# Expert rows stored in order and gathered per token, in place of scattered to their tokens, in a four-layer kernel on one core

## The chip, the cores and the metric

The kernel runs on one core of a Trainium2 chip. The metric is the device time of one execution in microseconds (us), the median of several runs. The engines are PE (matrix multiply, TensorE), DVE (VectorE), ACT (ScalarE), POOL (GpSimd) and SP (SyncE, here only an issuer of DMAs). Plain DMAs are issued by SP. DMAs that take row numbers from a tile (indirect DMAs) are issued by POOL.

## The reference, cut to what matters

4096 tokens of 256 values pass six steps, each with a residual. The change is in the first three mixtures (steps 1, 3 and 4).

```
x = x + 0.5 * MoE0(layernorm(x))     # 1
x = x + attention(layernorm(x))      # 2
x = x + 0.5 * MoE0(layernorm(x))     # 3
x = x + 0.5 * MoE1(layernorm(x))     # 4
x = x + mixer(layernorm(x))          # 5
x = x + 0.5 * MoE1(layernorm(x))     # 6
# MoE0: T = 4096 tokens, E = 8 experts; each takes its first T/E = 512 tokens, others get 0
idx = argmax(probs); locations = cumsum(mask) - mask; mask = mask * (locations < 512)
exp_out = einsum(exp_in, W) + b      # exp_in[e, c] is the token in slot c of expert e
out[token] = probs[token, idx] * exp_out[idx, its slot]
# MoE1: every token goes to expert e = argmax(gates)
h = gelu(x @ W1[e] + b1[e]); out = h @ W2[e] + b2[e]
```

## The kernel before, in words

All tokens stay in SBUF as `X` (128 partitions x 32 tiles x 256). Each of the six steps, here called stages, first makes layer norms of them, and the mixtures also choose experts (`pe_route`, `act_route`, `dve_route`, `pool_route`). In a route, DVE computes for each group of 8 tiles the slot number of every token, and POOL then sends the group's normalised rows to a DRAM area `moe0_slots` or `moe1_slots`, one indirect DMA per tile of 128 tokens (line L543, 32 of them per route). With each row go its token number and, for the last stage, its mean and deviation: two small POOL copies per group (L540, L541), so that a row is 259 wide.

In the expert stages (`*_moe0(r)`, `*_moe1(m)`), SP loads pairs of tiles from the slots into a ring of five (`rows`), PE transposes and multiplies, ACT and DVE move results, and DVE writes a pair of result tiles into a ring of three (`expert_out`, L678 and L862). MoE 0 has 16 pairs, MoE 1 has 20. POOL takes each pair as it is done and scatters it by the token numbers in the loaded rows to `expert_rows` in DRAM, one indirect DMA per tile (L716, semaphores `back0` to `back2`). The scatter's arrival frees both rings: SP loads pair j only when pair j - 5 is back (L570, L738), DVE writes pair n only when pair n - 3 is back. Slots that no token took hold a spare row number. For this the slots are filled from a tile `EMPTY` before each MoE 0: by SP at the start (L1560), and for the second time by way of an area `moe0_empty_slots` (stores L583, copied at L907 during attention). `expert_rows` is zeroed at L558.

When all pairs are back, SP (`sp_rows_back`, L608 to L612) reads `expert_rows` plainly into `normed` in five pieces of 4, 4, 8, 8 and 8 tiles (`y_in0` to `y_in4`). DVE of the next stage adds a tile times its gate to `X` (L287) just ahead of that tile's statistics (L308), so the first tiles can be worked on while the later ones land. It takes the statistics in groups: 4 tiles, then 8, 8, 8 and 4, or (4, 8, 4) in attention.

Each engine has its own program in order. At each stage's end every engine adds one to `stage_end`, and some steps of the next stage wait for all five:

- attention: only SP's loads of its weights (L892) and POOL. ACT and DVE then wait for the weights (`att_in`) to make `W1R` (L1101, L1184), and the projections (L980) follow.
- route2 (after the second MoE 0): ACT before the first copy of logits (L421, L422, `stage_end` 15).
- mixer: SP, ACT and DVE at their very beginning (L1385, L1442, L1489, `stage_end` 20).

Of the kernel before, what the change touches and what calls it, by code (L numbers as in the profile page):

```python
# [15 lines left out]
P = 128  # L16
# [82 lines left out]
def tiles_of(ap):  # L99
# [25 lines left out]
def plan(nc, a, out):  # L125
# [29 lines left out]
    k.SLOT = m.take("slot_of_token", [P, NT], I32)  # L155
    k.CE = m.take("tile_counts", [P, 4, E])
# [39 lines left out]
def plan_moe0(m, first):  # L196
    t = Names()
    t.LT = m.take("logits_T", [E, 3, 2 * P])
    t.WT = m.take("w0", [P, KD, E, D])
    t.BB = m.take("b0", [P, E, D])  # L200
    t.XS = m.take("rows", [P, RING_X, 2, RW])
    t.XST = m.take("rows_T", [P, 3, 2, KD, P])
    t.YS = m.take("expert_out", [P, 3, 2, D])
    t.EMPTY = m.take("empty", [P, NT, RW]) if first else None
    return t


def plan_moe1(m):
# [4 lines left out]
    t.XS = m.take("rows", [P, RING_X, 2, RW])  # L213
    t.HS = m.take("hidden", [P, 3, 2, D])
    t.YS = m.take("expert_out", [P, 3, 2, D])
    return t
# [63 lines left out]
def dve_add(k, stage, t):  # L280
# [4 lines left out]
    if t == CUTS[c][0]:  # L285
        nc.vector.wait_ge((s.y_in0, s.y_in1, s.y_in2, s.y_in3, s.y_in4)[c], 16 * n)
# [141 lines left out]
def dve_route(k, r):  # L428
# [18 lines left out]
    if r < 2:  # L447
# [75 lines left out]

def pool_route(k, r):
    nc, s = k.nc, k.s
    slots = k.slots0 if r < 2 else k.slots1
    number = k.XN[:, :, D:D + 1].bitcast(I32)[:, :, 0]
    if r == 1:
        nc.gpsimd.wait_ge(s.stage_end, 5 * 2)
        nc.gpsimd.wait_ge(s.slots_empty, 16)  # L530
    elif r == 2:
        nc.gpsimd.wait_ge(s.split_lo, 2 * KD)
    k.ps.step(nc.gpsimd.iota(number, pattern=[[P, NT]], base=0, channel_multiplier=1, allow_small_or_imprecise_dtypes=True))
    if r == 0:
        nc.gpsimd.wait_ge(s.emptied, 16 * E)
    for g in range(NG):
# [3 lines left out]
        nc.gpsimd.tensor_copy(k.XN[:, lo:hi, D + 1], k.MV[:, lo:hi, 0])  # L540
        k.ps.step(nc.gpsimd.tensor_copy(k.XN[:, lo:hi, D + 2], k.SD[:, lo:hi]))  # L541
        for t in range(lo, hi):
            nc.gpsimd.indirect_dma_start(out=slots, out_offset=bass.IndirectOffsetOnAxis(ap=k.SLOT[:, t:t + 1], axis=0),  # L543
                                         in_=k.XN[:, t, :], in_offset=None).then_inc(s.scattered, 16)
# [5 lines left out]
def sp_moe0(k, r):  # L550
# [6 lines left out]
    if r == 0:  # L557
        nc.sync.dma_start(tiles_of(k.y_rows[0:T, :]), t.EMPTY[:, :, 0:D]).then_inc(s.y0_zeroed, 16)  # L558
# [5 lines left out]
    back = (s.back0, s.back1, s.back2)  # L564
    pairs = NJ0 // 2
    for n in range(-3, pairs):
        j = n + 3
        if j < pairs:
            if j >= RING_X:
                nc.sync.wait_ge(back[(j - RING_X) % 3], back_count(r, j - RING_X))  # L570
# [10 lines left out]
        if r == 0 and n >= 0 and n % 2:  # L581
            cut = slice(n // 2 * NT * 2 // pairs, (n // 2 + 1) * NT * 2 // pairs)
            nc.sync.dma_start(tiles_of(k.empty0)[:, cut, :], t.EMPTY[:, cut, :]).then_inc(s.empty_stored, 16)  # L583
            if n == 1:
                nc.sync.dma_start(tiles_of(k.slots1[SPARE:SPARE + (NJ1 - NT) * P, :]),
                                  t.EMPTY[:, E:E + NJ1 - NT, :]).then_inc(s.spares_stored, 16)
    sp_rows_back(k, r)
    if r == 0:
        nc.sync.wait_ge(s.empty_stored, 16 * (pairs // 2))
        nc.sync.wait_ge(s.spares_stored, 16)  # L590
# [78 lines left out]
def dve_moe0(k, r):  # L669
    nc, s, t = k.nc, k.s, k.top0[r]  # L670
    back = (s.back0, s.back1, s.back2)
# [16 lines left out]
def pool_moe0(k, r):  # L688
    nc, s, t = k.nc, k.s, k.top0[r]
    xs_in = (s.xs_in0, s.xs_in1, s.xs_in2, s.xs_in3, s.xs_in4)  # L690
    pairs, at = NJ0 // 2, r * NJ0 // 2
    if r == 0:
# [9 lines left out]
        nc.gpsimd.wait_ge(s.y0_zeroed, 16)  # L702
    else:
        for sem in (s.y_in0, s.y_in1, s.y_in2, s.y_in3, s.y_in4):
            nc.gpsimd.wait_ge(sem, 16)
# [6 lines left out]
def pool_rows_back(k, t, n, to):  # L712
    nc, s = k.nc, k.s
    back = (s.back0, s.back1, s.back2)
    for i in range(2):
        nc.gpsimd.indirect_dma_start(  # L716
            out=to, out_offset=bass.IndirectOffsetOnAxis(ap=t.XS[:, n % RING_X, i, D:D + 1].bitcast(I32), axis=0),
            in_=t.YS[:, n % 3, i, :], in_offset=None).then_inc(back[n % 3], 16)
# [5 lines left out]
def sp_moe1(k, m):  # L724
    nc, s, t = k.nc, k.s, k.top1[m]
    xs_in = (s.xs_in0, s.xs_in1, s.xs_in2, s.xs_in3, s.xs_in4)
    back = (s.back0, s.back1, s.back2)
    nc.sync.wait_ge(s.pads_from, m + 1)
    for e in range(E):
        row = nc.sync.value_load(k.PADI[0:1, e:e + 1], min_val=0, max_val=SPARE - P)  # L730
        nc.sync.dma_start(k.slots1[bass.ds(row, P), :], k.PAD[:, e:e + RW]).then_inc(s.padded, 16)
# [4 lines left out]
    for j in range(NJ1 // 2):  # L736
        if j >= RING_X:
            nc.sync.wait_ge(back[(j - RING_X) % 3], back_count(m + 2, j - RING_X))  # L738
        for i in range(2):
            row = nc.sync.value_load(k.ROWI[0:1, 2 * j + i:2 * j + i + 1], min_val=0, max_val=SPARE + (NJ1 - NT - 1) * P)  # L740
            nc.sync.dma_start(t.XS[:, j % RING_X, i, :], k.slots1[bass.ds(row, P), :]).then_inc(xs_in[j % RING_X], 16)
    if m == 0:
        sp_rows_back(k, 2)
# [93 lines left out]
def dve_moe1(k, m):  # L837
# [5 lines left out]
    for n in range(pairs + 4):  # L843
        j = n - 4
        if 0 <= j < pairs:
            ys = t.YS[:, j % 3, :, :]
            bank = k.bank[6 + j % 2]
            if j >= 3:
                nc.vector.wait_ge(back[j % 3], back_count(m + 2, j - 3))
# [25 lines left out]
def pool_moe1(k, m):  # L875
    nc, s, t = k.nc, k.s, k.top1[m]
# [842 lines left out]
```

## Time and profile before

| | us |
|---|---|
| median of 3 runs | 1552.46 |
| the three runs | 1542.86, 1554.94, 1552.46 |
| the profiled execution, its own time | 1545.96 |
| its span, from the first to the last instruction | 1544.7 |
| PE, DVE, ACT, POOL busy | 1147.4, 973.6, 813.9, 606.7 |
| mean granted PE clock, as a share of full speed | 0.881 |

The chain of work that ended last is spread over many lines, since each stage has a bound of its own. The stages lie, in the span: route0 to 80 us, MoE 0 to 141, attention to about 920, route1 to 983, MoE 0 again to 1045, route2 to 1127, MoE 1 to 1247, mixer to 1350, route3 and MoE 1 again to the end. Work after 1350 is not touched by the change except for the DRAM area that it uses.

### The profile page before, as it was taken

The numbers are of one execution on the slowest core, as the hardware profiler recorded it, in microseconds if no ns is written. First come the engines' busy times: TensorE is split into PE (matmuls) and PEld (weight loads), VectorE is DVE, ScalarE is ACT, GpSimd is POOL, SyncE is SP. The second block draws the span as 40 slices with busy tenths as digits, with TensorE's granted clock in tenths as the row PEclk, the third lists the DMA queues.
The fourth block names the chain that finished last, engine by engine and source line by source line (L and its number), as shares of the span: only waits on it lengthen the run. The fifth ranks groups of instructions, "written<-read, shape, count | busy, mean of one in ns | idle before, by whom it ended". The sixth has DMA issues, their size and how long they took to land. (4 is left out here: it accounts for less than half of the span.)

```text
span 1544.7 us, 30156 instructions
## 1 busy us (share of the span) xinstructions
PE 1147.4 (74%) x12088; PEld 898.3 (58%) x12088; DVE 973.6 (63%) x1669; ACT 813.9 (53%) x907; POOL 606.7 (39%) x610
## 2 busy tenths in 40 slices
PE   4464789199999989649999967463669928973998
PEld 2253666188888886448888853352258814631786
DVE  4213745799999954689999984137424447743454
ACT  4311453499999804279999956134323324471332
POOL 2753000825545410435454445560723311335233
PEclk9888799699999999869999989696779968975898
DMA  9578101312122000101221221463333240013232
GB/s 293 217 220 251 44 1 34 135 57 85 56 84 82 31 8 1 58 28 57 84 80 61 84 79 70 149 219 116 114 90 101 90 147 0 1 41 129 66 101 79
DMA packets 84588, 140.55 MB, mean 91 GB/s; under 512 B 10574, under 2 KB 71246, under 8 KB 79956
## 3 DMA queue, kind: packets, MB, share of 16 engines
q1 hardware_dynamic: 71396, 102.76, 20.7%
q0 software_dynamic: 13056, 35.87, 6.5%
q8 instruction: 99, 1.62, 0.4%
q14 instruction: 37, 0.30, 0.1%
HBM read 86.60 MB, written 56.24 MB: 92 GB/s over the span
## 5 line engine op out<-in xcount | busy, mean ns | idle before, releaser
L1167 ACT ACTIVATE b_signs<-b_q_everywhere,normed 128x2048 bf16<-128x2048 f32 x224 | 432.7, 1993 | 32.0 <-PE bank L1077 27.2
L1077 PE MATMUL bank<-b_value_parts,b_signs 128*128 128x102 bf16 x8192 | 408.0, 209 | 36.5 <-DVE b_signs L1308 26.7
L1077 PEld LDWEIGHTS bank<-b_value_parts,b_signs 128*128 128x128 bf16 x8192 | 378.3, 97 | 73.3 <-DVE b_signs L1308 70.6
L1308 DVE TENSOR_SCALAR b_signs<-b_q_everywhere,normed 128x2048 bf16<-128x2048 f32 x288 | 390.7, 1392 | 1.9 <-PE bank L1077 1.9
L543 POOL DMA_INDIRECT moe_slots<-normed,slot_of_token x128 | 124.8, 975 | 39.3 <-issue 33.5
L1369 POOL TENSOR_TENSOR normed<-b_sums,normed 128x16 f32<-128x16 f32 x32 | 34.8, 1087 | 249.4 <-DVE b_sums L1319 249.4
L359 PE MATMUL bank<-identity,normed 128*128 128x128 f32 x256 | 51.6, 338 | 63.2 <-ACT normed L335 46.9
L1345 POOL TENSOR_TENSOR b_signs<-b_signs,normed 128x1024 f32<-128x1024 f32 x8 | 22.0, 2756 | 160.8 <-DVE normed L1258 160.3
L308 DVE BATCH_NORM_STATS2 ln_stats<-residual 128x6 f32<-128x256 f32 x192 | 73.8, 419 | 17.8 <-DMA bg<-in_bg 7.7
L1069 PE MATMUL bank<-normed,ones_bf 128*128 128x408 bf16 x128 | 28.9, 350 | 69.5 <-DVE normed L1276 69.5
L368 PE MATMUL bank<-normed_T,wg 128*8 128x256 f32 x256 | 75.9, 425 | 0.0
L359 PEld LDWEIGHTS bank<-identity,normed 128*128 128x128 f32 x256 | 33.6, 168 | 71.9 <-ACT normed L335 52.2
L1319 DVE TENSOR_REDUCE b_sums<-bank 128x136 f32<-128x408 f32 x128 | 72.5, 570 | 2.3 <-PE bank L1077 2.3
L716 POOL DMA_INDIRECT out_tokens<-f_expert_out,f_rows x40 | 38.4, 961 | 89.2 <-DVE f_expert_out L858 83.1
L716 POOL DMA_INDIRECT expert_rows<-d_expert_out,d_rows x40 | 38.9, 972 | 82.5 <-DVE d_expert_out L862 76.4
L335 ACT ACTIVATE normed<-residual,ln_shift,ln_rstd 128x256 f32<-128x256 f32 x128 | 68.6, 586 | 2.1 <-DVE ln_shift L330 2.1
L323 ACT ACTIVATE ln_std<-ln_mean_var,eps 128x4 f32<-128x4 f32 (+1 forms) x32 | 9.4, 293 | 109.7 <-DVE ln_mean_var L311 109.7
L1069 PEld LDWEIGHTS bank<-normed,ones_bf 128*128 128x128 bf16 x128 | 10.9, 99 | 75.8 <-DVE normed L1276 70.3
L678 DVE TENSOR_TENSOR a_expert_out<-bank,a_b 128x512 f32<-128x512 f32 x16 | 11.1, 692 | 63.3 <-PE bank L639 61.8
L1371 POOL TENSOR_TENSOR normed<-b_sums,normed 128x256 f32<-128x256 f32 x32 | 50.8, 1588 | 0.0
L872 DVE TENSOR_TENSOR f_rows_T<-bank,f_rows_T 128x512 fp32r<-128x512 f32 x20 | 13.8, 692 | 57.7 <-ACT f_rows_T L833 57.7
L1130 ACT ACTIVATE b_q_or_k_T<-bank 128x512 fp32r<-128x512 f32 x32 | 17.6, 595 | 60.1 <-PE bank L1006 60.1
(246 smaller groups left out, 2431.4 us busy)
## 6 DMA issues: line engine op xcount, KB each, us to landing
b_q_everywhere<-q_rows SPq DMA_DIRECT2D x32, 1024.0 KB, 4.7
normed<-expert_rows SPq DMA_DIRECT2D x9, 1024.0 KB, 10.3
d_rows<-moe_slots SPq DMA_DIRECT2D x40, 129.5 KB, 2.1
f_rows<-moe_slots SPq DMA_DIRECT2D x40, 129.5 KB, 2.1
moe_slots<-a_empty SPq DMA_DIRECT2D x8, 518.0 KB, 8.4
a_rows<-moe_slots SPq DMA_DIRECT2D x16, 259.0 KB, 3.6
moe_empty_slots<-a_empty SPq DMA_DIRECT2D x8, 518.0 KB, 5.3
moe_slots<-moe_empty_slots SPq DMA_DIRECT2D x1, 4144.0 KB
```

The source lines that it names most:

```text
L308: marks.append(k.vs.mark(nc.vector.bn_stats(k.STATS[:, t % 8, :], k.X[:, t, :])))
L335: return k.nc.scalar.activation(dst, k.X[:, t, :], ACT.Identity, bias=k.SHIFTS[:, t:t + 1], scale=k.RSTD[:, t:t + 1])
L359: ins = nc.tensor.transpose(k.bank[n % 3][:, (2 * c + i) * P:(2 * c + i + 1) * P], k.XN[:, 2 * n + i, c * P:(c + 1) * P], k.IDENT[:, :])
L368: ins = nc.tensor.matmul(k.bank[3 + p % 2][0:E, 0:2 * P], wg[:, c, :], k.XTR[:, p % 3, :, :, :].rearrange("p i k c -> p (i k c)")[:, c * 2 ...
L543: nc.gpsimd.indirect_dma_start(out=slots, out_offset=bass.IndirectOffsetOnAxis(ap=k.SLOT[:, t:t + 1], axis=0), in_=k.XN[:, t, :], in_offse ...
L716: nc.gpsimd.indirect_dma_start(out=to, out_offset=bass.IndirectOffsetOnAxis(ap=t.XS[:, n % RING_X, i, D:D + 1].bitcast(I32), axis=0), in_= ...
L1069: nc.tensor.matmul(bank[:, 0:QPB * VP].rearrange("p (i c) -> p i c", i=QPB), k.ONESB[:, :], t.HELD3[:, h, :].unsqueeze(1).broadcast_to([P, ...
L1077: ins = nc.tensor.matmul(banks[qt // QPB][:, qt % QPB * VP:(qt % QPB + 1) * VP], t.SG[:, (hh * TB + kt) % RING, qt * P:(qt + 1) * P], t.VO ...
L1167: nc.scalar.activation(t.SG[:, g % RING, :], t.QB[:, hh % 2, :], ACT.Sign, bias=t.NKT[:, kt, hh % H:hh % H + 1]).then_inc(s.sign_a, 1)
L1308: nc.vector.tensor_scalar(t.SG[:, g % RING, :], t.QB[:, hh % 2, :], t.KTM[:, kt, hh % H:hh % H + 1], 2.0, ALU.is_gt, ALU.mult).then_inc(s. ...
L1319: nc.vector.tensor_reduce(t.A[:, hh % 2, QPB * c:QPB * (c + 1), :], k.bank[4 * (hh % 2) + c][:, 0:QPB * VP].rearrange("p (i n c) -> p i c ...
L1371: step(nc.gpsimd.tensor_tensor(t.CT, t.A[:, r, :, 0:DH], q.unsqueeze(2).broadcast_to([P, TB, DH]), ALU.mult))
```

## The change

In the first three mixtures, SP stores each pair of result tiles plainly, one pair behind the other, to `moe0_rows` or `moe1_rows` (semaphores `stored0` to `stored2`). `rows` in the ring is freed when PE has transposed it, `expert_out` when its store has landed. DVE computes for every token the row where its result stands (`FROM`: two more operations in MoE 0, four in MoE 1). When all pairs are stored, POOL reads the rows back by these numbers, one indirect DMA per tile of tokens, 32 of them. They stand in POOL's program ahead of its `stage_end`. The last mixture still scatters to the output as before. Token numbers, means and deviations are written to the slots in the last route only, so rows are 256 wide elsewhere. Zeroing of `expert_rows`, the area of empty slots and its copy are gone, and `EMPTY` has 8 tiles in place of 32.

```diff
-    for n in range(-3, pairs):
-        j = n + 3
+    for n in range(-RING_X, pairs):
+        if n >= 0:
+            nc.sync.wait_ge(s.ys, at + n + 1)
+            nc.sync.dma_start(tiles_of(k.y0[2 * n * P:2 * (n + 1) * P, :]), t.YS[:, n % 3, :, :]).then_inc(stored[n % 3], 16)
+        j = n + RING_X
         if j < pairs:
             if j >= RING_X:
-                nc.sync.wait_ge(back[(j - RING_X) % 3], back_count(r, j - RING_X))
+                nc.sync.wait_ge(s.xs_turned, at + j - RING_X + 1)
...
-def sp_rows_back(k, m):
+def pool_rows_back(k, m, rows, where):
     nc, s = k.nc, k.s
-    for sem, n in zip((s.back0, s.back1, s.back2), back_all(m)):
-        nc.sync.wait_ge(sem, n)
+    for i, sem in enumerate((s.stored0, s.stored1, s.stored2)):
+        nc.gpsimd.wait_ge(sem, stored_count(m, max(j for j in range((NJ0, NJ0, NJ1)[m] // 2) if j % 3 == i)))
     if m == 1:
-        nc.sync.wait_ge(s.split_lo, 2 * KD)
+        nc.gpsimd.wait_ge(s.split_lo, 2 * KD)
     for sem, (lo, hi) in zip((s.y_in0, s.y_in1, s.y_in2, s.y_in3, s.y_in4), CUTS):
-        nc.sync.dma_start(k.XN[:, lo:hi, 0:D], tiles_of(k.y_rows[lo * P:hi * P, :])).then_inc(sem, 16)
+        for t in range(lo, hi):
+            nc.gpsimd.indirect_dma_start(out=k.XN[:, t, 0:D], out_offset=None, in_=rows,
+                                         in_offset=bass.IndirectOffsetOnAxis(ap=where[:, t:t + 1], axis=0)).then_inc(sem, 16)
...
 def pool_moe0(k, r):
-    for n in range(pairs):
-        nc.gpsimd.wait_ge(xs_in[n % RING_X], xs_count(r, n))
-        nc.gpsimd.wait_ge(s.ys, at + n + 1)
-        pool_rows_back(k, t, n, k.y_rows)
+    nc.gpsimd.wait_ge(s.rows_from, r + 1)
+    pool_rows_back(k, r, k.y0, k.FROM)
...
 def dve_moe0(k, r):
         if n >= 3:
-            nc.vector.wait_ge(back[n % 3], back_count(r, n - 3))
+            nc.vector.wait_ge(stored[n % 3], stored_count(r, n - 3))
...
 def pool_route(k, r):
-        nc.gpsimd.tensor_copy(k.XN[:, lo:hi, D + 1], k.MV[:, lo:hi, 0])
-        k.ps.step(nc.gpsimd.tensor_copy(k.XN[:, lo:hi, D + 2], k.SD[:, lo:hi]))
+        if r == 3:
+            nc.gpsimd.tensor_copy(k.XN[:, lo:hi, D + 1], k.MV[:, lo:hi, 0])
+            k.ps.step(nc.gpsimd.tensor_copy(k.XN[:, lo:hi, D + 2], k.SD[:, lo:hi]))
...
 def sp_attention(k):
-        if batch == 0:
-            nc.sync.dma_start(k.by_slot, k.empty0.rearrange("(e r) d -> e r d", e=E)).then_inc(s.slots_empty, 16)
```

## Rows read from the trace of the kernel before

**Rows 1.** Stretches of the two MoE 0 stages: busy us of each engine, clock, DMA share, GB/s.

```profile
91.10:136.30 45.20, 33.67 (x171) 26.34 (x169) 10.36 (x16) 9.32 (x15) 28.30 (x30) 1.00 0.79 244
991.80:1040.00 48.20, 34.87 (x171) 27.51 (x169) 19.50 (x19) 16.46 (x19) 33.09 (x29) 0.96 0.63 204
```

**Rows 2.** Waits, whole span: us in total, times, longest.

```profile
PE bank L627 <- DMA a_rows<-moe_slots: 36.8, 12, 26.3
...
SPq L572 <- DMA expert_rows<-a_expert_out,a_rows: 32.8, 10, 9.4
```

**Rows 3.** Timeline of first MoE 0: start, us, instruction [idle before].

```profile
90.44 0.69 DVE L678 TENSOR_TENSOR a_expert_out<-bank,a_b 128x512 f32<-128x512 f32 x1 [28.45 <-PE bank L639]
...
92.30 0.60 PE L627 MATMUL bank<-identity,a_rows 128*128 128x128 f32 x4
...
94.47 0.60 PE L627 MATMUL bank<-identity,a_rows 128*128 128x128 f32 x4
...
135.65 0.69 DVE L678 TENSOR_TENSOR a_expert_out<-bank,a_b 128x512 f32<-128x512 f32 x1 [1.45 <-DMA expert_rows<-a_expert_out,a_rows]
```

**Rows 4.** Timeline of POOL in route0, between two groups of scatters.

```profile
68.16 0.97 POOL L543 DMA_INDIRECT moe_slots<-normed,slot_of_token  x1 [0.31 <-issue]
69.13 0.21 POOL L540 COPY normed<-ln_mean_var 128x8 f32<-128x8 f32 x1
69.27 0.20 POOL L541 COPY normed<-ln_std 128x8 f32<-128x8 f32 x1
69.74 0.99 POOL L543 DMA_INDIRECT moe_slots<-normed,slot_of_token  x1 [0.28 <-POOL normed L541]
```

**Rows 5.** DMA issues of whole span: KB each, median us to landing.

```profile
a_rows<-moe_slots SPq DMA_DIRECT2D x16, 259.0 KB, 3.6
moe_empty_slots<-a_empty SPq DMA_DIRECT2D x8, 518.0 KB, 5.3
...
normed<-in_w SPq DMA_DIRECT2D x4, 1024.0 KB, 6.5
...
moe_slots<-pad_source SPq DMA_DIRECT2D x16, 129.5 KB, 2.5
...
e_scalars<-in_mix SPq DMA_DIRECT2D x1, 0.5 KB, 6.1
```

**Rows 6.** Timeline of SP, ACT and DVE where attention begins.

```profile
147.13 3.04 SPq L894 DMA_DIRECT2D b_wq<-in_wq  x1
...
169.69 0.69 DVE L1184 TENSOR_TENSOR b_hidden_weights<-b_q_everywhere,b_hidden_weights 128x512 fp32r<-128x512 f32 x1 [5.91 <-ACT b_hidden_weights L1101]
```

**Rows 7.** Timeline of SP and of ACT where the mixer and the sign steps begin.

```profile
1253.82 2.43 SPq L1386 DMA_DIRECT2D e_w_in<-in_win_t  x1
...
1259.20 0.43 SPq L1391 DMA_DIRECT2D e_scalars<-in_mix  x1
...
308.17 5.79 ACT L1167 ACTIVATE b_signs<-b_q_everywhere,normed 128x2048 bf16<-128x2048 f32 x3 [1.44 <-DVE b_value_parts L1268]
```

**Rows 8.** Timeline of second MoE 0 and route2, engine by engine.

```profile
1002.98 2.38 POOL L716 DMA_INDIRECT expert_rows<-c_expert_out,c_rows  x1 [0.59 <-issue]
...
1083.63 1.05 POOL L543 DMA_INDIRECT moe_slots<-normed,slot_of_token  x1 [0.30 <-issue]
...
991.09 0.69 DVE L678 TENSOR_TENSOR c_expert_out<-bank,c_b 128x512 f32<-128x512 f32 x1 [26.73 <-PE bank L639]
...
1002.23 2.29 DVE L684 TENSOR_TENSOR w_lo<-normed,w_hi 128x2048 fp32r<-128x2048 f32 x1
...
1039.35 0.69 DVE L678 TENSOR_TENSOR c_expert_out<-bank,c_b 128x512 f32<-128x512 f32 x1 [1.03 <-PE bank L639]
...
1068.53 0.37 ACT L422 ACTIVATE d_logits_T<-bank 8x256 f32<-8x256 f32 x1 [1.07 <-PE bank L368]
```

**Rows 9.** The tile of MoE 1's results: duration ns, first and last start.

```profile
L862 DVE COPY d_expert_out<-bank x20: 691/691/692, 1144.3 to 1242.6; 128x512 f32<-128x512 f32 x20
```

**Rows 10.** The chain that ended last, where the mixer begins.

```profile
1253.83 0.44 DVE residual L287
```

More of the change, by code:

```diff
@@ L155, in plan @@
     k.SLOT = m.take("slot_of_token", [P, NT], I32)
+    k.FROM = m.take("row_of_token", [P, NT], I32)
     k.CE = m.take("tile_counts", [P, 4, E])
@@ L200, in plan_moe0, with plan_moe1 @@
     t.BB = m.take("b0", [P, E, D])
-    t.XS = m.take("rows", [P, RING_X, 2, RW])
+    t.XS = m.take("rows", [P, RING_X, 2, D])
     t.XST = m.take("rows_T", [P, 3, 2, KD, P])
     t.YS = m.take("expert_out", [P, 3, 2, D])
-    t.EMPTY = m.take("empty", [P, NT, RW]) if first else None
+    t.EMPTY = m.take("empty", [P, NJ1 - NT, RW]) if first else None
     return t
-def plan_moe1(m):
+def plan_moe1(m, width):
     t = Names()
@@ L212, in plan_moe1 @@
     t.HT = m.take("hidden_T", [P, 2, 3, 2, KD, P], F32R)
-    t.XS = m.take("rows", [P, RING_X, 2, RW])
+    t.XS = m.take("rows", [P, RING_X, 2, width])
     t.HS = m.take("hidden", [P, 3, 2, D])
@@ L453, in dve_route @@
         k.vs.step(nc.vector.tensor_scalar(k.r_keep[:, :], k.r_slot[:, :], float(E * REGION + CAP), None, ALU.is_lt))
+        k.vs.step(nc.vector.tensor_scalar(k.r_slot[:, :], k.r_slot[:, :], float(E * REGION + CAP - 1), float(E * (CAP - REGION)),
+                                          ALU.min, ALU.add))
+        nc.vector.scalar_tensor_tensor(out=k.FROM[:, :], in0=k.r_rank[:, :], scalar=-float(CAP), in1=k.r_slot[:, :],
+                                       op0=ALU.mult, op1=ALU.add).then_inc(s.rows_from, 1)
         k.vs.step(nc.vector.tensor_tensor(k.r_gate[:, :], k.r_gate[:, :], k.r_keep[:, :], ALU.mult))
@@ L670, in dve_moe0 @@
     nc, s, t = k.nc, k.s, k.top0[r]
-    back = (s.back0, s.back1, s.back2)
+    stored = (s.stored0, s.stored1, s.stored2)
     pairs, at = NJ0 // 2, r * NJ0 // 2
@@ L688, in pool_moe0 @@
 def pool_moe0(k, r):
-    nc, s, t = k.nc, k.s, k.top0[r]
-    xs_in = (s.xs_in0, s.xs_in1, s.xs_in2, s.xs_in3, s.xs_in4)
-    pairs, at = NJ0 // 2, r * NJ0 // 2
+    nc, s = k.nc, k.s
     if r == 0:
@@ L727, in sp_moe1 @@
     back = (s.back0, s.back1, s.back2)
+    pairs, at = NJ1 // 2, m * NJ1 // 2
     nc.sync.wait_ge(s.pads_from, m + 1)
@@ L735, in sp_moe1 @@
     nc.sync.wait_ge(s.stage_end, 5 * (3, 5)[m])
[L736 to L743, printed above, removed]
+    for n in range(-RING_X, pairs):
+        if m == 0 and n >= 0:
+            nc.sync.wait_ge(s.m_ys, n + 1)
+            nc.sync.dma_start(tiles_of(k.y1[2 * n * P:2 * (n + 1) * P, :]), t.YS[:, n % 3, :, :]).then_inc((s.stored0, s.stored1, s.stored2)[n % 3], 16)
+        j = n + RING_X
+        if j < pairs:
+            if j >= RING_X and m == 0:
+                nc.sync.wait_ge(s.m_turned, j - RING_X + 1)
+            elif j >= RING_X:
+                nc.sync.wait_ge(back[(j - RING_X) % 3], back_count(j - RING_X))
+            for i in range(2):
+                row = nc.sync.value_load(k.ROWI[0:1, 2 * j + i:2 * j + i + 1], min_val=0, max_val=SPARE + (NJ1 - NT - 1) * P)
+                nc.sync.dma_start(t.XS[:, j % RING_X, i, :], k.slots1[m][bass.ds(row, P), :]).then_inc(xs_in[j % RING_X], 16)
 def pe_moe1(k, m):
@@ L847, in dve_moe1 @@
             bank = k.bank[6 + j % 2]
-            if j >= 3:
-                nc.vector.wait_ge(back[j % 3], back_count(m + 2, j - 3))
+            if j >= 3 and m == 0:
+                nc.vector.wait_ge((s.stored0, s.stored1, s.stored2)[j % 3], stored_count(2, j - 3))
+            elif j >= 3:
+                nc.vector.wait_ge(back[j % 3], back_count(j - 3))
             if m == 1:
@@ L876, in pool_moe1 @@
     nc, s, t = k.nc, k.s, k.top1[m]
+    if m == 0:
+        nc.gpsimd.wait_ge(s.rows_from, 3)
+        pool_rows_back(k, 2, k.y1, k.FROM)
+        return
     xs_in = (s.xs_in0, s.xs_in1, s.xs_in2, s.xs_in3, s.xs_in4)
-    pairs, at = NJ1 // 2, m * NJ1 // 2
-    for sem in (s.y_in0, s.y_in1, s.y_in2, s.y_in3, s.y_in4):
-        nc.gpsimd.wait_ge(sem, 32)
-    for n in range(pairs):
-        nc.gpsimd.wait_ge(xs_in[n % RING_X], xs_count(m + 2, n))
-        nc.gpsimd.wait_ge(s.m_ys, at + n + 1)
-        pool_rows_back(k, t, n, k.out if m else k.y_rows)
+    back = (s.back0, s.back1, s.back2)
+    for n in range(NJ1 // 2):
+        nc.gpsimd.wait_ge(xs_in[n % RING_X], xs_count(3, n))
+        nc.gpsimd.wait_ge(s.m_ys, NJ1 // 2 + n + 1)
+        for i in range(2):
+            nc.gpsimd.indirect_dma_start(
+                out=k.out, out_offset=bass.IndirectOffsetOnAxis(ap=t.XS[:, n % RING_X, i, D:D + 1].bitcast(I32), axis=0),
+                in_=t.YS[:, n % 3, i, :], in_offset=None).then_inc(back[n % 3], 16)
 def sp_attention(k):
@@ L1572, in sp_program @@
     sp_moe1(k, 1)
-    for sem, n in zip((s.back0, s.back1, s.back2), back_all(3)):
-        nc.sync.wait_ge(sem, n)
+    for i, sem in enumerate((s.back0, s.back1, s.back2)):
+        nc.sync.wait_ge(sem, back_count(max(j for j in range(NJ1 // 2) if j % 3 == i)))
 def pe_program(k):
```

93 lines of the change are left out of this document (39 added, 54 removed).

## The prediction

> **What bounds the kernel now.** I read the stretches first, then the waits, then the timelines of the three expert stages that the change touches and of what comes behind each. In both MoE 0 stages PE is busy for 33.7 and 34.9 us of 45.2 and 48.2 us, at nearly its full clock, and the DMA engines are 0.79 and 0.63 busy [rows 1]. So neither is the bound. The waits say what is: PE waits for loaded rows, and SP, which loads them, waits for scattered rows to come back [rows 2]. Where the rows are there, pairs follow each other at 94.47 - 92.30 = 2.17 us [rows 3]; from the first to the last result pair the stage takes 136.34 - 91.13 = 45.2 us for 15 steps, 3.01 us each [rows 3]. In the second MoE 0 it is 1040.04 - 991.78 = 48.3 us [rows 8]. Two scatters of 0.97 us with 0.31 us between them [rows 4] are 2.55 us per pair, more than PE's 2.17. In MoE 1 the pairs come at (1242.6 - 1144.3) / 19 = 5.17 us [rows 9], twice what POOL needs for its two scatters, so there nothing but the last pair is in the open.
>
> The change takes the scatter out of the loop and puts 32 gathers behind it, in front of a `stage_end`. So I must price the loops, and then the path from the last result to the first step that the gathers hold up. I take the stages one by one, each against the time of before.
>
> **Routes 0, 1 and 2.** The number, mean and deviation copies go. Between two groups POOL then needs 0.31 us in place of 69.74 - 69.13 = 0.61, and before the first group, by my estimate, 0.7 us less to do (two copies and their wait): three times 0.3 and 0.7 are 1.6 us in each route, as POOL works through all 32 scatters without a pause for slots. In route2 one group waits for its slots, so 1.4 there. Rows of 1024 in place of 1036 bytes change nothing, since POOL's own time sets the pace. The zeroing of `expert_rows` and the smaller `EMPTY` lie beside the scatters of route0, and the copy of empty slots lies in attention before the first sign step, which starts at 308.17 and waits for DVE and not for a DMA [rows 7]. I cost them at nothing; were that cover gone, the copy would be worth some 10 us of gain. DVE's two and four extra operations for `FROM` run while POOL scatters.
>
> **First MoE 0.** PE's pace becomes 2.17 us if the rest keeps up. Load n + 5 is now issued behind store n. It lands about 0.9 us (two issues) plus 3.6 us [rows 5] after result n, and PE needs it some 5.5 us after, so there is room. DMA traffic is 7 MB in 33 us, 215 GB/s, under the 244 / 0.79 = 309 that the engines showed [rows 1]. I take 2.2 us: 33.0 in place of 45.2 us. From the last result to the last store's landing I take 3.6 us. No such store is in the trace: 128 rows of 1 KB land in 2.5 us, 518 KB in 5.3 [rows 5]; the store is 256 KB, nearer to the first.
> Then 32 gathers. The trace has no gather. Its nearest row is the scatter, also 128 row numbers and 1 KB each: 0.97 + 0.31 = 1.28 us [rows 4], so 31 x 1.28 + 0.97 and a drain of 0.3 are 41.0 us. Below, a gather might be as cheap as a plain issue on SP, 0.43 us [rows 7], with the 0.31 between; above, 2.38 us, what a scatter took when DVE's 2.29 us operation ran beside it [rows 8]. I take the scatter, as it is the same kind of instruction.
> Who waits? ACT and DVE may start on the first tiles, which arrive early: 16 tiles have landed 16 x 1.28 + 2.5 = 23 us after the first gather, and ACT and DVE, by the order of their work before, are done with them some 16 us later, 39 us in all. But SP queues attention's eight loads behind `stage_end`, and ACT's and DVE's weight steps L1101 and L1184 need them. Six such loads for the mixer took 1259.63 - 1253.82 us to issue and 6.1 us to land, 11.9 us, with plain reads in front of them [rows 5, 7]; I take 11.5, and 0.7 for ACT. That is now the last: 33.0 + 3.6 + 41.0 + 11.5 + 0.7 = 89.8 us from the first result to L1184. Before it was 169.69 - 91.13 = 78.6 [rows 3, 6]. Loss 11.2, less 1.6 from route0: +9.6.
>
> **Second MoE 0.** Here SP also loads four raw weight pieces of 1 MB, 6.5 us each [rows 5]. Before, the first was issued ahead of the loop, since n ran from -3. Now it is issued behind result 1, and ACT wants it with pair 4, about 6.5 us later, while it lands 7.5 us or more after result 1 among stores and loads. Each piece then holds ACT (1.9 us of its own) and DVE (2.29, [rows 8]) up, and the next one is issued later. Following the four pieces I get 7.7 to 9 us per three pairs, in all 41 us in place of 48.3. Bounds: 33 us (PE's pace) and 48.3 (no gain).
> The waiting step behind the gathers is ACT's copy of logits in route2, before at 1068.53 [rows 8]: 76.8 us after the first result. Now: 41 + 3.6 + 41.0 = 85.6, +8.9. By then DVE has done the statistics of tiles 12 to 19, on which it was working before at that moment: -1.0. PE has stood idle and starts at half clock: +0.5. Routes: -1.6 and -1.4. Sum +5.4.
>
> **First MoE 1.** The loop stays PE's. Before, 10.5 us passed from the last result (1242.6 + 0.7) to the mixer's first step at 1253.83 [rows 9, 10], which waits for `stage_end`. Now 3.6 + 41.0 = 44.6 us. ACT, DVE and SP all wait there, so nothing of the gathers is hidden: +34.1.
>
> **Sum.** 9.6 + 5.4 + 34.1 = 49 us on the profiled execution's own time of 1545.96 (its span is 1544.7): 1595. The median of the three runs is 1552.46, 6.5 higher; on it the sum gives 1601.5. I predict 1600.
>
> **A rule of the skill beside it.** A 2.29 us DVE operation lengthened a scatter from 0.97 to 2.38 us; beside DVE's adds and statistics of route2 one took 1.05 [rows 8]. The Trainium skill, "GPSIMD Engine Reference", section "Key points", says that GpSimd shares its SBUF interfaces with VectorE and meets contention from instructions with two SBUF inputs; DVE's adds are such. If each of the 36 adds that run during the gathers of stages 1 and 3 cost a gather its own 0.47 us, the sum would be 17 us higher, near 1617. The row with 1.05 speaks for 3 us at most, and I leave it out.
>
> **Rivals.**
> *A gather is cheap* (not slower). If POOL hands over one description per tile and not 128 rows, a gather may cost what an issue on SP costs, 0.43 us, or 0.74 with the pause. Then each stage saves 32 x 0.54 = 17 us: 49 - 52 = -3, or 1550 on the median. The change decides between faster and slower at a step of 1.28 - 49/96 = 0.77 us. Against it: the scatter, with as many row numbers, is at 0.97 to 1.05 wherever DVE's long operation isn't beside it [rows 4, 8]. For it: only that the direction differs. Chance 0.06.
> *A gather is dear*: every one meets something like the 2.38 us scatter. 96 x 1.41 = 135 us more: about 1735. Half of that, 1670, would need contention on every second. In the mixer's case DVE is idle, which speaks against it. Chance 0.10. The Trainium skill's "GPSIMD Engine Reference", section "Performance pitfalls for Q7 kernels", has a harsher price, about 102 cycles for each small read command, such as one per gather index, not overlapped. It would apply to 128 indices, 13,000 cycles or some 10 us a gather, an estimate by that page, and 900 us in all. The scatter's 0.97 us for as many indices goes against it; I give it 0.01 of the 0.10.
> *The loops don't get faster*: loads queued behind stores come as late as scatters did before, and the pace stays 3.01 and 3.2 us. Loss 12.2 + 7.3: 49 + 19.5 = 69, about 1621. For it: the DMA engines were 0.79 busy, and SP is now in series behind result n. Against: the empty slots, 4 MB of the traffic, are gone. Chance 0.12.
>
> **How the numbers follow.** My forecast has 0.72. Its own range: cheaper by 8 (second MoE 0 at PE's pace), 3 (three stores at 2.5 us) and 2 (weight loads): +36; dearer by 2 for weight loads that queue as before, and 5 for stores at 5.3: +56. With the rival of the unchanged loops: +75. That is 1582 to 1621 on the profiled time and, with 6.5 for the median, up to 1628. The range 1582 to 1628 leaves out the cheap and the dear gather, 0.16. About 1 per cent is what a measurement of this kernel can tell from no change. Faster by over 1 per cent: only a gather well below the cheap rival's, 0.02. Within 1 per cent: 0.05. Slower: 0.93.
>
> **What would show it.** In the changed trace: POOL with three rows of 32 gathers at a step of 1.28 us, each followed by `stage_end`; results of the first MoE 0 at 2.2 us; ACT, DVE and PE idle for about 45 us ahead of the mixer; attention's weights landing some 11 us behind the last gather; w_hi steps that wait for raw weights. The prediction is wrong if a gather's step isn't near 1.28, or if the loops gain more than PE's pace allows, which they can't, or if a drain on POOL waits for data too, some 2 us per stage.

## The result and the profile after

The changed kernel takes 1606.6 us (median of 4 runs, 1604.6 to 1610.0), the kernel before 1552.3 (1542.9 to 1554.9): a ratio of 1.036, with a 95% interval of 1.032 to 1.040. The forecast was 1600 and slower. The profiled executions lie towards opposite ends of the spread (1610.0, the slowest after, and 1545.96, 6.5 under the median before), so their spans, 1608.5 and 1544.7, are 63.8 us apart where the medians are 54 apart.

The stretches of the changed kernel: first MoE 0 and second MoE 0 from the end of the first result to the end of the last, which answer to [rows 1], and the third from the last result of the first MoE 1 to the mixer's first add.

```profile
90.25:127.65 37.40, 33.34 (x171) 28.32 (x169) 10.38 (x15) 9.29 (x15) 0.00 (x0) 0.95 0.77 239
1004.78:1044.65 39.87, 34.09 (x171) 28.18 (x169) 18.99 (x19) 16.16 (x19) 0.00 (x0) 0.96 0.84 271
1273.89:1322.21 48.32, 0.00 (x0) 0.00 (x0) 0.00 (x2) 0.00 (x0) 30.52 (x32) 0.50 0.31 92
```

The loops fell from 45.2 to 37.4 and from 48.3 to 39.9 us, with POOL idle in them. In the third row POOL alone works, 30.5 us in 32 gathers of 48.3 us. The gathers as a group of the page, and DMA issues with their landing (the rows that answer to [rows 5]):

```profile
L630 POOL DMA_INDIRECT normed<-moe_rows,row_of_token x96 | 93.1, 970 | 260.3 <-DMA moe_rows<-d_expert_out 127.1
...
moe_rows<-d_expert_out SPq DMA_DIRECT2D x20, 256.0 KB, 2.2
...
moe_rows<-a_expert_out SPq DMA_DIRECT2D x16, 256.0 KB, 2.4
...
moe_rows<-c_expert_out SPq DMA_DIRECT2D x16, 256.0 KB, 3.8
...
normed<-moe_rows,row_of_token POOLq DMA_INDIRECT x96, 2.8
```

A gather is busy 0.97 us and lands 2.8 us after its issue. The Trainium skill, "Perfetto Trace Analysis", section "DMA Instruction — SWDGE (GPSIMD)", says that such an instruction ends in a profile when its descriptors are written, not when the data has moved; these two rows agree.

The timeline of the changed kernel from the last result of the first MoE 0 to attention's weights (it answers to [rows 3] and [rows 6]):

```profile
126.96 0.69 DVE L697 TENSOR_TENSOR a_expert_out<-bank,a_b 128x512 f32<-128x512 f32 x1 [1.04 <-PE bank L658]
130.59 0.99 POOL L630 DMA_INDIRECT normed<-moe_rows,row_of_token  x1 [49.97 <-DMA moe_rows<-a_expert_out]
131.89 0.96 POOL L630 DMA_INDIRECT normed<-moe_rows,row_of_token  x1 [0.30 <-issue]
...
170.38 0.95 POOL L630 DMA_INDIRECT normed<-moe_rows,row_of_token  x1 [0.30 <-issue]
176.66 0.37 SPq L909 DMA_DIRECT2D b_wq<-in_wq  x1
...
180.11 0.42 SPq L913 DMA_DIRECT2D b_bv<-in_bv  x1
...
183.39 0.63 ACT L1114 ACTIVATE b_hidden_weights<-b_q_everywhere 128x512 fp32r<-128x512 f32 x1 [14.99 <-DMA b_bv<-in_bv]
184.06 0.69 DVE L1197 TENSOR_TENSOR b_hidden_weights<-b_q_everywhere,b_hidden_weights 128x512 fp32r<-128x512 f32 x1 [21.01 <-ACT b_hidden_weights L1114]
```

The last gather ends at 171.33, but SP's first load, which waits for `stage_end`, goes out at 176.66, 5.3 us later. No instruction of any engine stands between: the chain puts this time down to POOL's drain (L1675). It comes again behind the other two rows of gathers:

```profile
1088.77 0.95 POOL L630 DMA_INDIRECT normed<-moe_rows,row_of_token  x1 [0.30 <-issue]
1095.10 0.37 ACT L423 ACTIVATE d_logits_T<-bank 8x256 f32<-8x256 f32 x1 [14.45 <-POOLq L1680]
...
1273.20 0.69 DVE L872 COPY d_expert_out<-bank 128x512 f32<-128x512 f32 x1 [3.74 <-PE bank L813]
...
1276.92 0.98 POOL L630 DMA_INDIRECT normed<-moe_rows,row_of_token  x1 [127.10 <-DMA moe_rows<-d_expert_out]
...
1315.93 0.95 POOL L630 DMA_INDIRECT normed<-moe_rows,row_of_token  x1 [0.30 <-issue]
1322.21 0.42 DVE L288 SCALAR_TENSOR_TENSOR residual<-normed,residual 128x256 f32<-128x256 f32 x1 [48.32 <-POOLq L1683]
```

5.4 us at ACT's first logits (they answer to 1068.53 in [rows 8]) and 5.3 us at the mixer's first add ([rows 10]). And the timeline of the first MoE 0 of the changed kernel where its pace breaks:

```profile
93.26 0.50 SPq L605 DMA_DIRECT2D moe_slots<-a_empty  x1
...
96.21 1.24 SPq L605 DMA_DIRECT2D last_slots<-a_empty  x1
98.12 0.69 DVE L697 TENSOR_TENSOR a_expert_out<-bank,a_b 128x512 f32<-128x512 f32 x1 [1.47 <-PE bank L658]
100.28 0.69 DVE L697 TENSOR_TENSOR a_expert_out<-bank,a_b 128x512 f32<-128x512 f32 x1 [1.47 <-PE bank L658]
105.82 0.69 DVE L697 TENSOR_TENSOR a_expert_out<-bank,a_b 128x512 f32<-128x512 f32 x1 [4.84 <-DMA moe_rows<-a_expert_out]
```

Results come every 2.16 us; then 5.5 us pass. I put this down to the stores and loads that queue behind two stores of spare rows, 1 MB each, which SP issues behind results 1 and 2 (counted from 0); a run below moves them away.

Where the 63.8 us between the spans lie (us; each row runs from the mark of the row above to its own):

| up to | before | after | difference | forecast |
|---|---|---|---|---|
| first result of MoE 0 (end) | 91.1 | 90.3 | -0.9 | -1.6 |
| DVE's weights of attention (L1184, now L1197) | 78.6 | 93.8 | +15.2 | +11.2 |
| first result of the second MoE 0 | 822.1 | 820.7 | -1.4 | -1.6 |
| ACT's first logits of route2 | 76.8 | 90.3 | +13.6 | +8.9 |
| first result of MoE 1 | 76.4 | 78.4 | +2.0 | -1.9 |
| its last result | 98.4 | 100.4 | +2.0 | 0 |
| the mixer's first add | 10.5 | 48.3 | +37.8 | +34.1 |
| the end | 290.9 | 286.3 | -4.6 | 0 |

### The profile page after: what moved, and what is told of

Same layout as the page of the kernel before. It is cut to its first block, busy times and chain, and to the rows that moved or that the text cites. A ratio compares the mean times of both kernels' runs of the same rounds, so it can differ in the third digit from the quotient of the medians.

```text
span 1608.5 us, 30095 instructions
## 1 busy us (share of the span) xinstructions
PE 1149.6 (71%) x12088; PEld 903.6 (56%) x12088; DVE 975.3 (61%) x1677; ACT 813.7 (51%) x907; POOL 584.1 (36%) x575
## 4 chain that ended last, share of the span: by engine, by line
PE 34%; DVE 32%; POOL 15%; issue 6%; POOLq 4%; DMA 4%; ACT 4%; SPq 1%; DVEq 0%; ACTq 0%
DVE b_signs L1321 21%; POOL moe_slots L563 5%; DVE b_sums L1332 4%; PE bank L810 4%; POOL normed L630 4%; PE bank L658 3%; PE bank L811 3%; PE bank L812 2%; PE bank L813 2%; PE bank L993 2%; PE bank L1090 2%; PE bank L1044 2%; DVE ln_stats L309 2%; POOL last_slots L563 2%; PE bank L1434 2%
## 5 line engine op out<-in xcount | busy, mean ns | idle before, releaser
L630 POOL DMA_INDIRECT normed<-moe_rows,row_of_token x96 | 93.1, 970 | 260.3 <-DMA moe_rows<-d_expert_out 127.1
L563 POOL DMA_INDIRECT moe_slots<-normed,slot_of_token x96 | 93.5, 974 | 102.8 <-DVE slot_of_token L499 74.5
L1422 PE MATMUL bank<-identity,normed_T 128*128 128x128 f32 x64 | 11.6, 319 | 70.5 <-ACT normed_T L336 70.4
L288 DVE SCALAR_TENSOR_TENSOR residual<-normed,r_gate,residual 128x256 f32<-128x256 f32 x64 | 30.2, 471 | 37.2 <-DMA normed<-moe_rows,row_of_token 37.2
L1422 PEld LDWEIGHTS bank<-identity,normed_T 128*128 128x128 f32 x64 | 8.3, 160 | 74.3 <-ACT normed_T L336 73.4
```

The lines of the kernel that those rows point to most:

```text
L630: nc.gpsimd.indirect_dma_start(out=k.XN[:, t, 0:D], out_offset=None, in_=rows, in_offset=bass.IndirectOffsetOnAxis(ap=where[:, t:t + 1], a ...
```

## The experiments

Each ran in several rounds beside the kernel before on the same chip, and ratios are to it, with 95% intervals. Four chips were used: A for the first four kernels (kernel before 1551.9 us), B for the next four (1572.4), C for the next three (1570.5), D for the last (1548.7). B and C are slower by more than a per cent; more on this below. Of all versions only the kernel before ran on all four, so a ratio on one chip set against a ratio on another can hold a difference of the chips.

**The gate ahead of the gathers.**

```diff
 def pool_rows_back(k, m, rows, where):
...
+    nc.gpsimd.drain().then_inc(s.stage_end, 1)
     for sem, (lo, hi) in zip(...):
...
     pool_moe0(k, 0)
-    nc.gpsimd.drain().then_inc(s.stage_end, 1)
```

> The changed kernel with one thing moved, in all three stages: POOL's drain and its stage_end stand behind the waits for the stores and ahead of the 32 gathers. Theory A (the gathers cost so much since a stage_end stands behind them, and a drain): attention's weights, route2's logits and the mixer start as soon as the stores have landed. I expect 14 us less ahead of attention, 14 ahead of route2 and 31 ahead of the mixer, 1606.6 - 59 = 1548 us, within 0.5 per cent of the kernel before. If the drain costs its 5.3 us also where no indirect DMA ran shortly before, 16 us more: 1564. Theory B (the rows come late whatever the gate does, since one gather takes 1.26 us and DVE waits for 16 tiles): less than 20 us gained, above 1586.

Measured: 1573.2 us, ratio 1.016 (1.013 to 1.018). 33 us of the loss went with the place of the gate: `stage_end` had held steps up that need none of the gathered rows. That is between the two theories, for two reasons. The drain costs something here too: in the first MoE 0, 5.7 us passed from the last result's end to the first gather (126.99 to 132.70), and 2.9 in the changed kernel. The length of the drain itself stands on its line, 2.65 and 2.68 us in the two MoE 0 stages and 5.26 in MoE 1:

```profile
L626 POOLq DRAIN  x3: 2651/2680/5264, 129.2 to 1251.7; - x3
```

And what the gate lets go meets the gathers' own pace. The chief row of waits for the add:

```profile
DVE residual L288 <- DMA normed<-moe_rows,row_of_token: 66.3, 9, 15.1
```

In the changed kernel the same row has 37.2 us.

**A no-operation in place of the drain.** In it POOL's sequencer runs ahead of the engine, so `stage_end` is no longer behind the gathers.

```diff
     pool_moe0(k, 0)
-    nc.gpsimd.drain().then_inc(s.stage_end, 1)
+    nc.gpsimd.nop().then_inc(s.stage_end, 1)
```

> The changed kernel with a nop in place of each of the three drains that stand behind the gathers; nothing else. Theory A: the 5.3 us from the end of the last gather to stage_end are the drain's own, so 3 x 5.3 = 16 us go: 1591 us. Rival: POOL's queue gives the signal no sooner than the last gather's descriptors or data are done with, whatever instruction carries it: 1606, no change.

Measured: 1562.0 us, ratio 1.009 (1.006 to 1.011). Far more than either theory gave, as both took the signal for one that comes behind the last gather. SP's first load and DVE's weights among the gathers:

```profile
153.54 0.37 SPq L909 DMA_DIRECT2D b_wq<-in_wq  x1
153.78 0.95 POOL L630 DMA_INDIRECT normed<-moe_rows,row_of_token  x1 [0.30 <-issue]
...
157.95 0.43 SPq L918 DMA_DIRECT2D b_sums<-in_bk  x1
...
166.37 0.69 DVE L1197 TENSOR_TENSOR b_hidden_weights<-b_q_everywhere,b_hidden_weights 128x512 fp32r<-128x512 f32 x1 [5.91 <-ACT b_hidden_weights L1114]
```

The signal came at 153.5, between gathers 20 and 21 (the last starts at 168.19): 12 gathers ahead of the end, and so it was in the MoE 1 stage. DVE's weights came at 166.37 in place of 184.06, ACT's first logits at 1063.27 in place of 1095.10. The drain's price isn't gone, though: the next drain, at the end of attention, was 0.04 us long in the changed kernel and is 5.30 here, 745 us behind the last gather. Nothing waits for it there: from DVE's weights to the first scatter of route1 it took 770.5 us here and 769.5 in the changed kernel.

**MoE 0 alone.** The first MoE 1 scatters as before (`out_offset` by the token number, the ring freed by `back`), the two MoE 0 stages store and gather.

> The change in the two MoE 0 stages alone; the first MoE 1 scatters its rows by token number and reads them plainly, as before (rows of 259 with their number there). Theory A: ahead of the mixer nothing of the gathers was hidden and nothing gained, so all of the 37.8 us that the trace shows there go, and 2 us of the loop: 1606.6 - 39 = 1567 us. Theory B (the mixer would have waited for its rows or weights anyway): less than 20 us less, above 1586.

Measured: 1568.8 us, ratio 1.012 (1.009 to 1.014). A is right: of 3.6% loss the MoE 1 stage holds 2.5, or 38 us, where the table has +37.8 for the way to the mixer's first add.

**Spare rows stored in route0.**

```diff
     if r == 0:
         for n in range(2):
+            nc.sync.dma_start(tiles_of(k.slots1[n][SPARE:...]), t.EMPTY[...]).then_inc(s.spares_stored, 16)
...
-        if r == 0 and n in (1, 2):
-            spares = tiles_of(k.slots1[n - 1][SPARE:...])
```

> The changed kernel with the two stores of spare rows (2 MB) issued in route0, ahead of the first MoE 0's loop, in place of between its stores and loads. Theory A: these two transfers made the one stall of the loop (4.8 us before the result at 105.8), and without them pairs come at 2.17 us from first to last, 33 in place of 37.4 us: 1602 us. Rival: the stall is the loop's own (a store waits its turn behind loads whatever else is queued): still there, 1606.

Measured: 1600.4 us, ratio 1.032 (1.029 to 1.035). A is right. The loop went from 88.29 to 120.24, 32.0 us: PE's pace without a break.

**The kernel before without the drain's price.** The same edit as above, three times, in the kernel before. The timeline and the chain of the kernel before, where the mixer begins:

```profile
1247.84 5.54 SPq L612 DMA_DIRECT2D normed<-expert_rows  x5
...
1253.83 0.43 DVE L287 SCALAR_TENSOR_TENSOR residual<-normed,residual 128x256 f32<-128x256 f32 x1 [10.49 <-POOLq L1676]
```

```profile
1246.34 1.52 issue
1247.86 5.94 POOLq L1676
```

> The kernel before with one edit: POOL still waits for all scattered rows, but a plain no-operation, not a drain, adds to stage_end behind the first three mixtures. Theory A (a drain on POOL behind indirect DMAs costs about 5.9 us of its own, although the rows are back): it stands ahead of attention's weights, of route2's first logits and of the mixer, so up to 3 x 5.9 = 18 us go: 1534 to 1541. Rival B (the 5.9 us are time in which the data still settles, or other work hides the drain in the two MoE 0 stages): 1546 to 1552.

Measured: ratio 0.999 (0.996 to 1.002). B's number, by its second reason, and in all three stages: other work lies beside the drain. The same rows without the drain:

```profile
1269.25 5.55 SPq L612 DMA_DIRECT2D normed<-expert_rows  x5
1274.89 0.43 DVE L287 SCALAR_TENSOR_TENSOR residual<-normed,residual 128x256 f32<-128x256 f32 x1 [10.14 <-SPq L1569]
```

SP's five plain reads take 5.5 us to issue, and SP's own signal stands behind them. The wait is put down to SP now and is as long, 10.1 for 10.5 us. In the two MoE 0 stages it is alike: from the last result to attention's weights 33.4 us passed with the drain and 33.1 without, to ACT's first logits in route2 28.5 and 28.5. All three drains can be read in the trace of before, on their own lines:

```profile
L1664 POOLq DRAIN  x1: 5293/5293/5293, 141.2 to 141.2; - x1
...
L1666 POOLq DRAIN  x1: 34/34/34, 917.2 to 917.2; - x1
...
L1671 POOLq DRAIN  x1: 5274/5274/5274, 1045.7 to 1045.7; - x1
...
L1676 POOLq DRAIN  x1: 5933/5933/5933, 1247.9 to 1247.9; - x1
```

So the drain was there before, of about the same size, and free; the change took away the reads that covered it. As above, the no-operation only put the price off: the drain at the end of attention (L1666) took 5.29 us without the first of them, where it hid as well.

**Plain reads of the stored rows.** The 96 gathers are left out, and SP reads the areas in five pieces, in the experts' order.

```diff
-        for t in range(lo, hi):
-            nc.gpsimd.indirect_dma_start(out=k.XN[:, t, 0:D], ...)
+        nc.sync.dma_start(k.XN[:, lo:hi, 0:D], tiles_of(rows[lo * P:hi * P, :])).then_inc(sem, 16)
```

> The changed kernel without its 96 gathers: SP reads the stored rows plainly in five pieces, as before, so the rows stay in the experts' order and the output is another one. It prices the rest of the change alone. Theory A (the loops gain what the traces show): 1552 - 4.6 (routes) - 7.8 and - 8.4 (the two MoE 0 loops) - 15 (POOL's drain now stands behind nothing) = 1516, and the gathers with their drains then cost 1606 - 1516 = 90 us. Rival B (the loops' gain is given back where rows are read back, since stores and plain reads queue behind one another): 1535 or more.

Measured: ratio 0.984 (0.981 to 0.987), 26 us on 1572, between the two. The loops gave what A took (37.4 and 40.6 us from the first result's start to the last's, against 46.5 and 47.9 in the kernel before with the no-operation, on the same chip): 16 us. A's 15 for POOL's drain weren't there, as the run above shows. So the gathers and what waits for them cost some 1.0364 - 0.9837 = 5.3%, 82 us, and the loops and routes give 26 back; the first ratio is from another chip than the second.

**A wait for the data, then the drain.**

```diff
+    for sem, (lo, hi) in zip((s.y_in0, s.y_in1, s.y_in2, s.y_in3, s.y_in4), CUTS):
+        nc.gpsimd.wait_ge(sem, 16 * (hi - lo) * (m + 1))
     nc.gpsimd.drain().then_inc(s.stage_end, 1)
```

> The changed kernel with one edit: behind its 32 gathers POOL waits until all of them have landed, and only then comes the drain. Theory A (the drain has a cost of its own, some 5.5 us, that runs beside the landing of 2.7 to 3.7 us where nothing is waited for): the landing comes on top, 3 x 3 = 9 us more than the changed kernel: 1616. Rival B (the drain only waits until the gathers' data is in): it is short once they have landed, and the time stays at 1607 to 1609.

Measured: ratio 1.044 (1.041 to 1.048). The chain behind the first row of gathers:

```profile
173.97 0.95 POOL normed L630
174.92 1.81 issue
176.74 0.04 POOLq L633
176.78 0.04 issue
176.82 5.30 POOLq L1677
```

A is right: all rows are in at 176.8, and the drain still takes 5.30 us (5.28 in the third stage). It doesn't wait for data. The wait for the rows added 1.9 us in each stage, 5.7 in all, not A's 9.

**What the drain's length goes by.** No run was made for this, but the traces show it. The length goes by the number of indirect DMAs, gathers and scatters alike, that POOL has issued since its drain before:

| indirect DMAs since the last drain | where | drain, us |
|---|---|---|
| 0 | end of attention, before and changed | 0.03, 0.04 |
| 32 | with the gate first: both MoE 0 stages, end of attention | 2.65, 2.68, 2.66 |
| 64 | before, both MoE 0 stages; gate first, MoE 1; waited for, all three | 5.29, 5.27; 5.26; 5.29, 5.27, 5.27 |
| 72 | before, MoE 1 (its 40 scatters and route2's 32) | 5.93 |

That is 0.082 us for each, from 32 on. In the changed kernel 64 stand before each of the three drains, the 32 scatters of the route and the 32 gathers. It fits up to 72 only: behind no-operations, with 128 or 136 since the last drain, the one at the mixer's end took 6.6 us (128) and 4.6 and 9.5 us (136), where it takes 1.4 behind none. Why isn't known.

**Three edits together: MoE 0 alone, no-operation, spare rows early.**

> Three of the separate edits together: stored rows and gathers in MoE 0 alone (first MoE 1 scatters as before), a no-operation in place of POOL's drain in all three stages, and the two spare-row stores moved to route0. Theory A (their effects add): 1568.8 of the MoE 0 only version, less 6.2 for the spare rows, less 17.7 and 14.1 that the no-operation gave in the two MoE 0 stages, less 5.9 for the drain ahead of the mixer = 1525, faster than the kernel before. Rival B (the gates and the spare rows gain the same time twice, and the tiles that come back at 1.26 us each set the pace of the next statistics): 1540 to 1555.

Measured on chip B: ratio 1.008 (1.005 to 1.010). B's side, and no better than the no-operation alone had been on chip A. Its trace showed what no trace of chip A has: towards the end of each row of gathers the other engines' instructions come further apart. So the two were run side by side, on chip C.

> The changed kernel with a no-operation in place of POOL's drain behind the gathers once more, now beside the combined version on the same chip. Theory A (the gain of 45 us was the kernel's and not the chip's): ratio to the kernel before again 1.006 to 1.012. Rival B (on a chip where the other engines pause beside POOL's indirect DMAs, as the traces of the third group of runs showed, it gains less): 1.018 or more.

> Stored rows and gathers in MoE 0 alone, a no-operation in place of the drain, spare rows early, once more, beside the version with the no-operation alone. Theory A (the effects add, and the 1.0075 of the first time came from the pauses on that chip): 1552 - 8 (stage 1 ahead of before by 3 us, spare rows 5 more) - 2 = 1542, ratio 0.990 to 0.997, and below the version beside it by 1.2% or more. Rival B (they gain the same time twice): equal to the version beside it within 0.5%, and above 1.003.

Measured on C: the no-operation alone 1.032 (1.029 to 1.036), the combined version 1.006 (1.004 to 1.008). For the first, rival B: most of the gain of chip A is a gain of that chip. For the second neither: the version is 2.6% below the one beside it, as A said, but above the kernel before, as B did. The timeline of SP, as attention's loads are issued with the no-operation, first on chip A, then on C:

```profile
156.01 0.47 SPq L911 DMA_DIRECT2D b_bp<-in_bp  x1
156.52 0.43 SPq L912 DMA_DIRECT2D b_bp<-in_bp  x1
157.00 0.42 SPq L913 DMA_DIRECT2D b_bv<-in_bv  x1
```

```profile
168.11 0.70 SPq L911 DMA_DIRECT2D b_bp<-in_bp  x1
169.50 0.70 SPq L912 DMA_DIRECT2D b_bp<-in_bp  x1
170.91 0.70 SPq L913 DMA_DIRECT2D b_bv<-in_bv  x1
```

0.5 us a load on A, 1.4 us on C, from 168 us on, some 28 us after the first gather. It ends with the gathers. In the stretch before it and in it, first on C, then in the like stretches on A, busy times and numbers of instructions of PE, of its weight loads, of DVE, ACT and POOL, then clock, DMA share and GB/s:

```profile
139.00:168.00 29.00, 2.12 (x9) 1.46 (x9) 13.12 (x44) 3.73 (x9) 21.64 (x23) 0.50 0.38 108
168.00:180.00 12.00, 3.29 (x13) 2.12 (x12) 2.18 (x9) 3.33 (x7) 9.25 (x10) 0.50 0.63 193
```

```profile
128.00:156.00 28.00, 1.66 (x7) 1.26 (x8) 12.62 (x43) 3.27 (x8) 21.60 (x22) 0.50 0.37 106
156.00:168.00 12.00, 7.86 (x29) 5.24 (x28) 4.47 (x14) 9.97 (x21) 9.14 (x10) 0.50 0.70 203
```

In 12 us DVE, ACT and PE get 9, 7 and 13 instructions done on C, and 14, 21 and 29 on A, while POOL keeps its 10 gathers on both. What holds them is open. The kernel before has no gathers, but on B (with the no-operation) its rows of scatters in the four routes are longer too: 44.5, 44.2, 47.7 and 47.2 us from the first to the last start, for 40.7, 40.4, 41.7 and 40.6 in the trace of before. In route1, for one, POOL waits 2.7 us for slots of DVE ahead of the third group, and not at all in the trace of before. These 20 us are nearly all of the 22 between the two spans. Whether it is the same pause isn't shown.

**A ring slot more in the kernel before.** No edit of the change is in it: `RING_X` 6 for 5, the results' ring 4 for 3, with a semaphore for each slot (run on C).

> The kernel before, scatter and all, with one ring slot more on each side: six pairs of loaded rows in place of five, four pairs of results in place of three (and a semaphore for each). It asks whether the loops of MoE 0 need the new way of storing at all. Theory A (the pace of 3.0 and 3.2 us is the round trip of a pair, some 15 us, over five slots): it becomes 15 / 6 = 2.5, held at 2.6 by POOL's two scatters, so 15 steps take 39 to 40 us in place of 45.2 and 48.3; 1552 - 14 = 1538. Rival B (a scatter's own traffic and the loads get slower as more are under way, or MoE 1 loses): 1548 or more.

Measured: ratio 0.996 (0.994 to 0.997), 7 us. It is the only version with all its work that beats the kernel before, and by less than 1%. The loops took 42.3 and 44.4 us, counted as with the plain reads, not 39 to 40 (46.5 and 47.9 in the kernel before with the no-operation, on B, a chip like C): half of what A expected.

**The changed kernel again**, on D.

> The changed kernel itself once more, unaltered, as the version with the no-operation came out at 1.0086 on the one chip and at 1.0322 on the other. Theory A (the pauses of the other engines hit what runs beside the gathers, and with the drain in place nearly nothing of value runs there, so the changed kernel loses the same on both chips): ratio to the kernel before 1.034 to 1.041, and a no-operation gains only some 0.7% on such a chip. Rival B (the pauses lengthen the changed kernel too): 1.050 to 1.060, and the no-operation keeps a good part of its 2.8%.

Measured: 1605.6 us, ratio 1.038 (1.036 to 1.041). But D turned out to be a chip without the pauses (kernel before 1548.7), so it confirms the result and doesn't tell A from B. The run that waits for the data speaks for A: it had 1.044 on B, and without its own 5.7 us it would be at 1.041, by my estimate, near the 1.036 and 1.038 of the chips without pauses.

## Why the prediction was right

The forecast was +48 us on the median and +49 on the profiled time; it is +54 on the medians and +64 between the two profiled executions. Terms that were too small and too large made up for one another in part, so the nearness on the medians is partly luck. Its mechanism holds: the loops gain, the gathers stand in the open ahead of three `stage_end`, and the MoE 1 stage pays most. By its steps:

- *A gather costs 1.28 us.* 0.95 + 0.30 = 1.25 to 1.26. 32 of them took 40.7, 40.7 and 40.0 us for 40.7 forecast. The rivals of a cheap and of a dear gather are out. So is the 102 cycles for each index of the Trainium skill's "GPSIMD Engine Reference", section "Performance pitfalls for Q7 kernels": no gather of the changed kernel took over 1.20 us for its 128 indices.
- *A drain of 0.3.* This is the term that was mis-sized: 5.3, 5.4 and 5.3 us, 16 in place of 0.9. The forecast named the possibility ("if a drain on POOL waits for data too, some 2 us per stage") with too small a price and another cause. The rows for it were in the trace of before, 5.29, 5.27 and 5.93 us on the drains' own lines; I had read the chain there only for the add.
- *First loop 33.0.* 37.4. The stores of spare rows, which I left out, cost 5.4: with them moved it was 32.0, a little under the forecast.
- *Second loop 41.* 39.9; the raw weights held ACT and DVE up as described.
- *Stores of 3.6 us.* 2.9, 4.3 and 3.0 from the last result to the first gather.
- *Weights of attention 11.5.* 6.7 (176.66 to 183.39). With nothing ahead of them on SP's queue the eight loads went out in 3.9 us. This error of -4.8 hid the drain's +5.0 in that stage.
- *Contention with DVE.* By the Trainium skill's "GPSIMD Engine Reference", section "Key points", as I had priced it, 17 us. The gathers' mean is 0.970 us, and undisturbed ones take 0.95: 2 us in all, inside the 3 that I took from the trace.
- *Loops that don't get faster.* Out: both did, by 7.8 and 8.4 us.
- *Route2, MoE 1 and the end.* +2.0, +2.0 and -4.6 where I had -1.9, 0 and 0. No run was made for these, but the traces speak for the spread between executions and not for the change. In the changed kernel on D the same route2 took 74.0 us for 78.4, with a granted clock of 0.73 as before and not 0.65; at the same clock it is about 2.5 us shorter than before. With the spare rows moved, MoE 1 took 98.3 (98.4 before) and the way behind the add 290.5 (290.9 before).

## What to carry to other kernels

Before work is moved out of a loop and behind it, ask what signal it will stand in front of: here each MoE 0 loop gained 8 us and its stage lost 14 or 15 all the same, and MoE 1 lost 38, since a `stage_end` that most of its waiters didn't need for these rows came behind 32 gathers. A drain that is free today may be free only because something as long runs beside it; read its own length on its line before taking that cover away, and count the indirect DMAs since the drain before. A further drain behind each route's scatters, beside work that doesn't need it, might leave 2.65 us of the 5.3 in the open, an estimate from the rows with 32; no run tried it. And a gain that comes from work beside a row of indirect DMAs needs a second chip before it is believed.

## What the runs showed of the hardware

- A drain on POOL takes 0.03 to 0.04 us with no indirect DMA since the last drain, 2.65 to 2.68 with 32, 5.26 to 5.30 with 64 and 5.93 with 72, some 0.082 us for each. It is the same when their data is in already (5.30 and 5.28) and when the last of them lies 745 us back (5.30): a no-operation put it off to the end of attention and did not save it.
- A no-operation behind the gathers signals when 12 of 32 are still to be worked through. Where the next stage must not start before the gathers end, it is no substitute.
- A gather of 128 rows of 1 KB costs POOL what a scatter does, 0.95 to 0.97 and 0.30 us, and lands in 2.7 to 3.7 us. The Trainium skill, "DMA: Bandwidth & Descriptors", section "Anatomy of one DMA — SWDGE (gpsimd) path", has 2.0 us and bytes / 436e3, by my estimate 2.3 us for 128 KB; the trace is above it.
- On two of four chips the other engines slowed to one instruction per 1.4 us or so from about 28 us into a row of gathers to its end, while POOL kept its pace. The kernel before was 1.2 to 1.3% slower on these chips than on A; in the one trace of it compared, 20 of 22 us lie in its four rows of scatters.
